# Four fused blocks of a small transformer on one core: a new written-out order of all five engines, three finer waits, and query blocks written over all 128 partitions

## The reference, cut to what matters

```python
x = x + autocorrelation(layernorm(x), ctx, ctx)   # 8 heads, top 9 lags per column, softmax over them
x = x + lora_experts(layernorm(x))                # x @ W_base.T + b, plus 2 of 8 experts of rank 16
x = x + window_attention(layernorm(x), ctx)       # channels = the 128 rows, 8 heads of 16, window of 16 along 1024
x = x + lora_experts_2(layernorm(x))              # 2 of 4 experts of rank 16, no base product
```

## Time and profile before

| | |
|---|---|
| median of three runs | 1871.96 us (1867.45 to 1872.3) |
| span of the profiled execution | 1867.4 us, 48204 instructions |
| busy PE, PEld | 1708.1 us (91%), 1082.9 us (58%) |
| busy DVE, ACT, POOL | 1569.8 (84%), 1165.5 (62%), 905.9 us (49%) |
| chain that ended last | PE 56%, DVE 19%, ACT 9%, POOL 8%, issue 6% |
| mean granted clock of TensorE | 0.971 of full speed |

### The profile page before, as it was taken

The page is one execution under the profiler, slowest core; times in us unless marked ns, Lnnn a source line. Parts: engine busy times, 40 slices in busy tenths (PEclk is TensorE's granted clock), DMA queues, the critical chain, the costliest instruction groups (busy, mean ns, idle before and its releaser), DMA issues.

```text
span 1867.4 us, 48204 instructions
## 1 busy us (share of the span) xinstructions
PE 1708.1 (91%) x19296; PEld 1082.9 (58%) x19296; DVE 1569.8 (84%) x4726; ACT 1165.5 (62%) x1929; POOL 905.9 (49%) x870
## 2 busy tenths in 40 slices
PE   3689999999999999999999999999999999999975
PEld 2356566666556666556666655666665566665553
DVE  6778898888889888888888888988888888888853
ACT  5257666666666665765666676666666566667642
POOL 2445544455554545555455555444555545455432
PEclk8799999999999999999999999999999999999985
DMA  5133322333332233332223333223334322333220
GB/s 208 34 58 69 58 50 48 54 69 69 69 48 47 54 61 69 69 58 53 48 51 69 69 69 57 49 48 55 69 69 64 51 48 48 67 69 58 29 30 24
DMA packets 549359, 111.37 MB, mean 60 GB/s; under 512 B 531088, under 2 KB 531344, under 8 KB 548624
## 3 DMA queue, kind: packets, MB, share of 16 engines
q1 hardware_dynamic: 549136, 108.29, 30.7%
HBM read 57.94 MB, written 16.78 MB: 40 GB/s over the span
## 4 chain that ended last, share of the span: by engine, by line
PE 56%; DVE 19%; ACT 9%; POOL 8%; issue 6%; DMA 1%; SPq 0%; DVEq 0%; ACTq 0%; POOLq 0%
PE pb L601 18%; PE pc L674 8%; ACT q_diag L876 6%; POOL rest L1422 4%; PE pa L561 4%; POOL prob L1422 4%; PE pa L523 3%; PE pa L497 3%; PE pa L524 3%; PE pa L498 3%; PE pa L499 3%; ACT v_im L778 3%; PE pb L590 2%; DVE rows_c L1249 2%; DVE x_c L1141 2%
## 5 line engine op out<-in xcount | busy, mean ns | idle before, releaser
L601 PE MATMUL pb<-w_base_h,even_words 128*128 128x512 f16 x1024 | 324.8, 379 | 0.0
L1459 POOL TENSOR_TENSOR sc<-sc,sc_rec 128x512 f32<-128x512 f32 x128 | 134.1, 1048 | 294.6 <-DVE sc_rec L1236 294.6
L876 ACT ACTIVATE q_diag<-sc,par 32x512 f32<-32x512 f32 x384 | 268.8, 715 | 10.3 <-DVE sc L1149 3.1
L1429 POOL TENSOR_TENSOR p_hl<-sc,p_hl 128x512 f16<-128x512 f32 x128 | 164.3, 1283 | 208.0 <-ACT p_hl L778 208.0
L601 PE MATMUL pb<-w_base_l,even_words 128*128 128x512 f16 x512 | 193.9, 379 | 0.0
L488 PE MATMUL pa<-xn_a,tab 128*128 128x512 f32 x384 | 181.7, 610 | 4.6 <-ACT xn_a L778 4.6
L674 PEld LDWEIGHTS pc<-sc_t,v_diag 128*128 128x128 f16 x6144 | 170.1, 97 | 20.6 <-DVE sc_t L1243 6.0
L674 PE MATMUL pc<-sc_t,v_diag 128*128 128x32 f16 x6144 | 173.9, 177 | 5.6 <-DVE sc_t L1243 5.6
L652 PE MATMUL pc<-k_h,q_diag 128*128 128x32 f16 x2048 | 169.2, 177 | 0.0
L653 PE MATMUL pc<-k_l,q_diag 128*128 128x32 f16 x2048 | 168.5, 177 | 0.0
L654 PE MATMUL pc<-k_h,q_diag 128*128 128x32 f16 x2048 | 168.5, 177 | 0.0
(11 more groups left out here) (166 smaller groups left out, 4619.6 us busy)
## 6 DMA issues: line engine op xcount, KB each, us to landing
x_a<-in_x SPq DMA_DIRECT2D x32, 512.0 KB, 5.5
x_res<-in_ctx_in SPq DMA_DIRECT2D x32, 512.0 KB, 5.1
x_res<-in_x SPq DMA_DIRECT2D x32, 512.0 KB, 3.7
v_diag<-even_words SPq DMA_DIRECT2D x128, 128.0 KB, 4.9
v_diag<-p_hl SPq DMA_DIRECT2D x128, 128.0 KB, 4.9
out<-rows_c SPq DMA_DIRECT2D x32, 512.0 KB, 2.6
v_diag<-in_base_w SPq DMA_DIRECT2D x4, 1024.0 KB, 10.0
q_diag<-in_ra SPq DMA_DIRECT2D x1, 544.0 KB, 13.7
```

The source lines that it names most:

```text
L601: mm(pb[:, h, :], rows[:, cols], weights[:, j, h * HALF:(h + 1) * HALF], start=(j == 0 and m == 0), stop=False)
L876: nc.scalar.activation(q_diag[rows, blocks, col:col + QB], source, ACT.Copy, scale=par[rows, a:a + 1]).then_inc(qd_out.sem, 1)
L1429: g_.tensor_tensor(part[:, :, :, LO], sc[:, g % 2, :, :], part[:, :, :, HI], ALU.subtract)\
```

## The change

All five `step` functions are written anew. In batches relative to the step of PE (a batch's name by its age: U the youngest, T one older, S two, R three):

- **PE**: `a_context_long` 0 of U now follows both halves of `a_corr`, not the first; `a_context_long` 1 of a batch and `c_scores` 2 stand behind the next `b_router`, not ahead of it; `c_attend` 0 stands behind a quarter of the base product, and `b_keys` behind `c_scores` 3. From `b_values` to `c_scores` 1 the order is as before.
- **DVE**: of stage c's group 2 the sums come ahead of the gates, `c_subtract` 3 ahead of `c_transpose` 1; the statistics of the next x (`a_norm`) move from behind `b_values_low` to behind `a_product`, a batch earlier; `b_values` 0 comes ahead of `b_base`; `c_norm_rows` comes behind `a_products` 0, not behind 1; the rows of norm 1 come ahead of `c_scores` 0; `c_result` 1 comes later, and so does `c_transpose` 0; `a_lead` comes near the end of the step, behind both `a_top`.
- **ACT**: `a_exp` 0 stands between the two `a_values_long`; `a_exp` 1 ahead of `c_high` 2; `a_values` stands behind four query blocks after `experts_mid`, not behind six; the features' copies of T stand among the query blocks of the second half.
- **POOL**: `b_bias` stands behind the second `c_low`; all four query blocks stand together at the end; six waits on its own semaphores are gone.
- **SP**: `load_x_res` behind the first four placing DMAs, the load of the next x behind that of the next ctx.
- **Finer waits**: `v_placed` is two semaphores, one for each half; `b_values` 0 waits for a new `mm_base` (the base product's second parts) in place of `mm_ffn`; waits for constants move into the functions that need them. `c_subtract` 2 and 3 gain a wait for `pl_out`.
- **Query blocks**: each instruction writes one head's 16 columns over all 128 partitions, times a 0/1 column `own` that is 1 on the head's rows; ACT has heads 0 to 5, POOL heads 6 and 7, 12 and 4 instructions per batch as before. `clear_queries` is gone.

```diff
-        v_placed = signal("v_placed", 16 * 2 * PAIRS)
-        qd_out = signal("qd_out", 4 * (PAIRS - 1))
+        v_placed = [signal(f"v_placed{n}", 16 * PAIRS) for n in range(2)]
+        qd_out = signal("qd_out", 2 * (HEADS - 2))
...
-                        mm(pb[:, h, :], rows[:, cols], weights[:, j, h * HALF:(h + 1) * HALF],
-                           start=(j == 0 and m == 0), stop=False)
+                        last = mm(pb[:, h, :], rows[:, cols], weights[:, j, h * HALF:(h + 1) * HALF],
+                                  start=(j == 0 and m == 0), stop=False)
+                if part == 1:
+                    last.then_inc(mm_base.sem, 1)
...
-            def b_query_blocks(b, pair, a, half):
-
-                if pair == 0 and a == 0:
+            def b_query_blocks(b, head, half):
+
+                if head == 0:
                     act.wait_ge(ql_out.sem, ql_out.after(b))
...
-                nc.scalar.activation(q_diag[rows, blocks, col:col + QB], source, ACT.Copy,
-                                     scale=par[rows, a:a + 1]).then_inc(qd_out.sem, 1)
+                nc.scalar.activation(q_diag[:, blocks, head * QB:(head + 1) * QB],
+                                     q_hl.rearrange("p (n t) -> p n t", t=QB)[:, blocks], ACT.Copy,
+                                     scale=own[:, head:head + 1]).then_inc(qd_out.sem, 1)
...
-                    dve.wait_ge(mm_ffn[0].sem, mm_ffn[0].after(b))
+                    dve.wait_ge(mm_base.sem, mm_base.after(b))
```

DVE's new list, from the gates of S on (i-3 there is S, i-4 is R, i-2 is T, i-1 is U):

```diff
+                    gates(i - 3, 0, pb, E0)
+                    c_scores(i - 4, 3)
+                    c_subtract(i - 4, 3)
+                    c_transpose(i - 4, 1)
+                    b_keys(i - 3)
+                    c_sums(i - 4, 3)
+                    c_transpose(i - 4, 2)
+                    a_ninth(i - 2)
+                    c_transpose(i - 4, 3)
+                    a_softmax(i - 2)
+                    b_values_low(i - 3)
+                    variance(i - 1, 0)
+                    b_values(i - 3, 0)
+                    b_base(i - 3)
+                    mean(i - 3, 2, x2_out)
+                    c_attention_residual(i - 4)
+                    mean(i - 4, 3, x3_out)
+                    b_norm_rows(i - 3, 2)
+                    a_products(i - 2, 0)
+                    c_norm_rows(i - 4)
+                    a_products(i - 2, 1)
+                    a_products(i - 2, 2)
+                    a_products(i - 2, 3)
+                    b_values(i - 3, 1)
+                    b_queries(i - 3)
+                    gates(i - 4, 1, pc, E1)
+                    a_residual(i - 2)
+                    c_result(i - 4, 0)
+                    b_norm(i - 2, 1, x1_out)
+                    variance(i - 2, 1)
+                    b_norm_rows(i - 2, 1)
+                    c_scores(i - 3, 0)
+                    c_subtract(i - 3, 0)
+                    a_product(i - 1)
+                    a_norm(i)
+                    b_features(i - 2, 0)
+                    c_sums(i - 3, 0)
+                    b_features(i - 2, 1)
+                    c_scores(i - 3, 1)
+                    c_subtract(i - 3, 1)
+                    c_result(i - 4, 1)
+                    a_top(i - 1, 0)
+                    c_sums(i - 3, 1)
+                    a_top(i - 1, 1)
+                    c_transpose(i - 3, 0)
+                    a_lead(i - 1)
+                    c_scores(i - 3, 2)
```

More of the change, by code:

```diff
@@ L412, in load_x, with next_x, next_ctx @@
                 sp.dma_start(x_a[:, :], x[b]).then_inc(x_in.sem, 16)
+            def next_x(b):
+                if not early(b):
+                    load_x(b)
+            def next_ctx(b):
+                if not first(b):
+                    load_ctx(b)
             def load_x_res(b):
@@ L463, in step @@
                 if live(1):
-                    load_x_res(i - 1)
-                if live(2):
[L466 to L472, removed]
+                    next_x(i - 1)
+                if live(5):
+                    store(i - 5)
+                if live(3):
+                    place_values(i - 3, 0)
+                if live(2):
+                    load_x_res(i - 2)
                 if live(3):
-                    store(i - 3)
-            for i in range(BATCH + 4):
+                    place_values(i - 3, 1)
+                if live(0):
+                    next_ctx(i)
+            for i in range(BATCH + 5):
                 step(i, during(i))
@@ L664, in c_attend @@
                 if g == 0:
-                    pe.wait_ge(v_placed.sem, v_placed.after(b))
+                    pe.wait_ge(v_placed[0].sem, v_placed[0].after(b))
+                    pe.wait_ge(v_placed[1].sem, v_placed[1].after(b))
                     if not first(b):
@@ L758, in step @@
                     a_corr(i, 0)
-                    a_context_long(i, 0, odd)
                     a_corr(i, 1)
[L761 to L772, removed]
+                    a_context_long(i, 0)
+            for i in range(BATCH + 3):
+                step(i, during(i))
         @block.scalar
@@ L812, in a_values_long, with spread @@
                 copy([v_re, v_im][n][:, :], pa_hi).then_inc(vagg_out.sem, 1)
-            def spread(b, n, rows, place, slot):
+            def spread(b, n, rows, place):
                 act.wait_ge(ln_part[n].sem, ln_part[n].after(b))
@@ L820, in spread @@
                     act.wait_ge(pt_out.sem, pt_out.after(b))
-                nc.scalar.activation(place[:, :], rows[:, slot, :] if n == 2 else rows[:, :], ACT.Square, bias=ln_lead[n][:, :], scale=-D ** -0.5,
+                nc.scalar.activation(place[:, :], rows[:, b % 2, :] if n == 2 else rows[:, :], ACT.Square, bias=ln_lead[n][:, :], scale=-D ** -0.5,
                                      accum_out=mv[n][:, 1:2]).then_inc(ln_mv[n].sem, 1)
@@ L837, in b_features @@
                 if h == 0 and not first(b):
-                    act.wait_ge(v_placed.sem, v_placed.after(b - 1))
+                    act.wait_ge(v_placed[0].sem, v_placed[0].after(b - 1))
                 act.wait_ge(tr_x[0].sem, tr_x[0].after(b, h + 1))
@@ L899, in c_high @@
                 if g == 0:
-                    act.wait_ge(v_placed.sem, v_placed.after(b))
+                    act.wait_ge(v_placed[1].sem, v_placed[1].after(b))
                 act.wait_ge(p_out.sem, p_out.after(b, g + 1))
@@ L1287, in step @@
                 if live(0):
-                    a_lead(i)
+                    a_norm(i)
                 if live(2):
-                    c_transpose(i - 2, 1)
-                    c_subtract(i - 2, 3)
-                if live(1):
-                    b_keys(i - 1)
-                if live(2):
-                    c_sums(i - 2, 3)
-                    c_transpose(i - 2, 2)
-                if live(0):
-                    a_ninth(i)
-                if live(2):
-                    c_transpose(i - 2, 3)
@@ L1361, in step @@
-                if live(1):
-                    c_transpose(i - 1, 0)
-                    c_sums(i - 1, 1)
-                    c_scores(i - 1, 2)
-                if live(-1):
-                    a_top(i + 1, 1)
+                    a_lead(i - 1)
+                if live(3):
+                    c_scores(i - 3, 2)
             v.memset(rs_power[:, :], -0.5).then_inc(power_set.sem, 1)
@@ new lines, in step @@
+                if live(2):
+                    root(i - 2, 2)
+                if live(3):
+                    root(i - 3, 3)
+                if live(1):
+                    a_sum(i - 1, 0)
+                    a_sum(i - 1, 1)
+                if first(i - 1):
+                    clear_values()
+                if live(2):
+                    b_query_blocks(i - 2, 6, 0)
+                    b_query_blocks(i - 2, 7, 0)
+                    b_query_blocks(i - 2, 6, 1)
+                    b_query_blocks(i - 2, 7, 1)
@@ L1526 @@
+            pool.wait_ge(power_set.sem, 3)
+            for i in range(BATCH + 3):
+                step(i, during(i))
 _OUTS = [((32, 128, 1024), "float32")]
```

358 lines of the change are left out of this document (151 added, 207 removed).

## The result

Slower: 1878.48 us, median of four runs (1875.95 to 1879.07), beside 1870.68 for the kernel before in four runs on the same chip (1867.45 to 1872.3). The ratio is 1.0043, 95% interval 1.003 to 1.0055. The profiled executions have spans of 1876.4 and 1867.4 us.

A forecast was written before the change was run, and what follows sets the result against it. PE was taken to bound the kernel, about 51.3 of 55 us a period. +0.19 us over 30 periods (+5.7), start -2.9 and end -3.1 gave -0.3 us: 1871.7 us; own range 1865 to 1879, all rivals 1857 to 1888.

The forecast's parts named there:

- `c_norm_rows`, +0.37: DVE's norm rows behind the first product: third product and POOL's sums end later, +0.37 us a period.
- chain 1: Dependent steps from `c_output` through DVE, ACT and POOL to PE's second aggregate: 13.13 us before, predicted 13.50.
- PE's 0.19 us of idle for these rows goes: PE's wait for `c_norm_rows` was to vanish, with its weight loads' share of it: 0.19 us.
- same: Outcome class for the whole kernel's time, 1866.3 to 1877.6 us, which held the forecast; chance 0.40.
- Chain 2, -0.31: From the second aggregate to `a_corr`, 11.27 us before: earlier norm rows start the product sooner, -0.31 us a period.
- Query blocks, 0: ACT's blocks over 128 partitions instead of 32 were to take the same 0.72 us each: 0.
- New front, +0.13: DVE's added statistics and sums behind the product make `c_transpose` 1 late for PE's `c_attend` 1, +0.13 us a period.
- Finer base wait, 0: `b_values` 0 frees 1.2 us of DVE ahead of the attention residual, but PE's `c_output` was tied: gain 0.
- Start, -2.9: Into batch 1's first `a_corr`: norm rows freed from POOL's clearing, -6.6; second x's wait, +3.2; stated as -2.9 us.
- End, -3.1: Last router comes earlier as DVE's features end sooner and group 2's scores move behind it, -3.1 us.
- Rival 1: Next x lands late for DVE's statistics, +0.6 us a period, 1890 us; chance 0.28.
- Rival 2: DVE's norm rows of stage c cost nothing, +0.37 goes to 0, 1861 us; chance 0.22.

The follow-up runs named there:

- experiment 1: The changed kernel with `c_norm_rows` alone put back behind `a_products` 1 in DVE's list: 1855.02 us, ratio 0.9916 to the kernel before.
- experiment 3: The kernel before with only `c_norm_rows` moved behind `a_products` 0: 1892.5 us, ratio 1.0114 to the kernel before.
- experiment 2: The changed kernel with three useless matmuls into a free bank between router and first aggregate: 1868.94 us, ratio 0.9989 to the kernel before.
- experiment 6: Experiment 5 with `b_values` 0 behind `b_base` again, its wait for `mm_base` kept: 1848.38 us, ratio 0.989 to the kernel before.
- experiment 5: The changed kernel with `c_norm_rows` back behind `a_products` 1 and `c_scores` 0 back ahead of norm 1's rows: 1843.05 us, ratio 0.9857 to the kernel before.
- experiment 4: The kernel before with only the query blocks changed, each written for one head over all 128 partitions: 1849.72 us, ratio 0.9888.

## Why the prediction was wrong

The mechanisms that I named were mostly there. What made it "slower" was one that I had no term for.

- **`c_norm_rows`, +0.37:** chain 1 is 13.58 us for 13.13, +0.45, and experiments 1 and 3 give 0.45 and 0.46. The marks were right: DVE idle 0.36 us ahead of the rows, PE's wait for them gone. The wait for the second sum grew not to 0.7 but to 0.33, because 0.61 went to the first.
- **The failed step: "PE's 0.19 us of idle for these rows goes", with nothing said of where PE's idle goes.** Before, PE's pauses lay apart: one for the rows, one for the router, one for the sums. Now the one for the rows is gone, pauses of 0.74 and 0.61 us stand with only the router between them, and the clock fell in every third or fourth period. That costs 7.5 us in the middle and about 9 in all (experiment 2). With the second pause filled the kernel took 1868.94, which is within my "same" and 2.8 us from the forecast.
- **Chain 2, -0.31:** measured -0.20 (11.07 us for 11.27). I gave the maximum and the subtraction 0.61 us each in any order; with its subtraction waiting directly behind it the first takes 0.72.
- **Query blocks, 0: wrong by the most.** I read that 128 partitions cost no more than 32 on POOL and stopped there. On ACT they cost less. Duration hardly tells: 710 ns beside 720. The row of six does: the spacing is (3.78 - 0.71) / 5 = 0.61 us, beside 0.72. Worth -0.635 us a period alone, 21 us. In the changed kernel it gained little, since two other moves took 0.45 each: 54.965 - 0.635 + 0.45 + 0.45 = 55.23, the measured period. My +0.19 for +0.265 was right for reasons that were partly wrong: I credited the order of four blocks instead of six with the gain that faster blocks brought, and missed that this order left the chain with DVE.
- **New front, +0.13:** nothing. PE shows no wait ahead of `c_attend` 1.
- **Finer base wait, 0:** right for a normal period, 5.3 us wrong over the kernel in experiment 6. I looked only for a wait of PE, not at when SP's loads start.
- **Start, -2.9:** the first `a_corr` of batch 1 came at 74.81 us for 77.79, -3.0. The number fits better than its working: -6.6 and +3.2 make -3.4, and not the -2.9 that I wrote. Both parts are in the trace. DVE waits at the second x, and the norm rows go free:

```profile
28.86 1.29 DVE L1037 BATCH_NORM_STATS2 small<-x_a 128x6 f32<-128x512 f32 x2 [10.23 <-DMA x_a<-in_x]
...
67.38 1.23 DVE L1129 TENSOR_TENSOR x_b<-pa,x_res 128x1024 f32<-128x1024 f32 x1 [7.28 <-PE pa L570]
68.64 1.29 DVE L1037 BATCH_NORM_STATS2 small<-x_b 128x6 f32<-128x512 f32 x2
...
71.36 0.81 DVE L1054 TENSOR_SCALAR xn_b<-x_b,small 128x1024 f32<-128x1024 f32 x1 [1.19 <-POOL small L1415]
```

```profile
63.63 6.92 POOL L1477 MEMSET v_diag<- 128x8192 f32 x1
```

  The residual and the statistics lie inside the clearing (to 70.55) and take their usual 1.23 and 1.29 us. That settles what no row of before could: the Trainium skill ("SBUF — State Buffer", section "Who interferes with whom") has them run freely there, and the trace agrees. Of the 3.0 us 1.9 were lost again by the third second aggregate, where PE's clock also fell once.
- **End, -3.1:** measured -5.1, right in sign; experiments 1, 2 and 5 end the same way (-4.4, -4.6, -6.5).
- **Rival 1 (x late, slower)** got the sign and not the cause: in none of the 29 periods has DVE a wait for a DMA above 0.15 us. It was close: x lands 9.4 us behind the second aggregate (median; the latest at 11.0), and DVE asks for it at 10.9. Experiment 6 shows its mechanism at work in four periods. Its time, 1890 us, lay outside the range of 1857 to 1888 that was to hold all rivals. **Rival 2** priced the kernel without the cost of `c_norm_rows` at 1861; with that step undone it took 1855.0, since the long periods went too.

The steady period was inside my 55.0 to 55.4, and the time inside my range. The sum was 7 us low on the medians and 9.3 on the span. Of these 9.3, 7.5 are the clock's in the middle, 2.0 the normal periods (7.7 for 5.7) and 1.8 the start (-1.1 for -2.9), against 2.0 more won at the end.

## What to carry to other kernels

Where a reordering shifts PE's waits, look not only at their sum but at whether two of them now lie close together: pauses of 0.7 us that cost nothing themselves can cost 1 us of slow clock, and a few matmuls into a free bank show in one run whether they do. Price a run of short instructions on one engine from the spacing of their starts, not from the mean duration, and watch whether neighbours use the same partitions. Look along all periods, not at one: a move that does nothing in a normal period can still decide whether a load comes in time in the others. And when a change bundles several moves, undo them one at a time: here one part was worth -21 us, two others cost 23 and 12 us together with it, and the whole looked like nothing.

## What the runs showed of the hardware

- **ACT, changing rows:** blocks of 512 elements per partition start 0.61 to 0.63 us apart when they follow one on the same partitions and 0.73 to 0.75 us apart when they change to another group of 32. In the totals a change adds 0.13 us (4.31, 4.18 and 3.78 us for six blocks with four, three and no change). The Trainium skill ("ScalarE: Activation LUTs", section "What ACT_TABLE_LOAD costs") has back-to-back activations overlap by 93 ns. The blocks of experiment 4 agree, 710 ns long and 614 apart; those of the kernel before, 720 long and 718 apart in the mean, hardly overlapped.
- **TensorE's clock** fell to 1.2 GHz behind two pauses of 0.74 and 0.61 us, 2.6 us from one's end to the other's, in every third or fourth of otherwise equal periods. With three matmuls (0.81 us) in the second pause it stayed at 2.4 GHz throughout the middle. Why one period in three or four, and not each, no run here shows.
